# First attention of an eight-sequence transformer: when the loads that fill the stacked queries and keys are issued, and what the long loads and zeros wait for

## The reference, cut to what matters

```
q, k, v = (x @ W.T + b), 16 heads of 8;  heads 0-7 and 8-15 form two groups
a  = softmax(q k^T * 8**-0.5)                         # 512 x 512 per head and sequence
out = concat([x1 - lv * x2, x2]) @ Wp.T + bp          # first attention
top-2 of 8 experts with capacity, pre * silu(gate)    # first expert layer
causal attention, 16 heads of 64                      # second attention
top-4 of 8 experts and a shared expert                # second expert layer
```

## Time and profile before

| | before |
|---|---|
| timed, median of 3 (range) | 1605.11 us (1603.35 to 1608.68) |
| profiled execution, its time | 1597.47 us |
| its span, first to last instruction | 1596.1 us |
| PE busy | 1491.6 us (93%) |
| DVE busy | 1085.2 us (68%) |
| ACT busy | 953.4 us (60%) |
| first attention, about | 52 to 505 us of the span |

### The profile page before, as it was taken

How to read it: one execution, slowest core, us unless ns; L and a number is a source line. 1 busy time by engine, 2 the same in 40 slices (tenths; PEclk the granted TensorE clock), 3 DMA queues, 4 the chain that set the end, 5 groups by cost and what they waited for, 6 DMA issues and landing times.

```text
span 1596.1 us, 26780 instructions
## 1 busy us (share of the span) xinstructions
PE 1491.6 (93%) x8976; PEld 886.4 (56%) x8976; DVE 1085.2 (68%) x3464; ACT 953.4 (60%) x2490; POOL 757.9 (47%) x1250
## 2 busy tenths in 40 slices
PE   4899898899898999998999999999999999998999
PEld 2333333333334999986556565656555565655566
DVE  5887898898793577644776767676777777673333
ACT  4577677777675433444776667575776757573221
POOL 7313354454435677564553646363554534342332
PEclk7798999999998999999999999999999999999999
DMA  6557764683514566872000000000000000020322
GB/s 152 68 125 128 121 138 94 104 134 112 84 35 163 172 194 211 268 234 73 5 12 1 15 1 15 1 15 1 8 8 3 13 1 2 1 54 1 93 67 53
DMA packets 76029, 118.95 MB, mean 75 GB/s; under 512 B 18795, under 2 KB 39533, under 8 KB 75885
## 3 DMA queue, kind: packets, MB, share of 16 engines
q0 software_dynamic: 33952, 67.69, 20.1%
q1 hardware_dynamic: 41504, 48.76, 10.8%
q10 hardware_dynamic: 436, 0.79, 0.2%
HBM read 77.84 MB, written 39.45 MB: 73 GB/s over the span
## 4 chain that ended last, share of the span: by engine, by line
PE 59%; DVE 14%; ACT 10%; DMA 8%; POOL 5%; issue 3%; ACTq 0%; POOLq 0%; DVEq 0%
PE bank L1344 6%; ACT ar L1572 6%; PE pS L1311 5%; DMA dm<-xT 5%; PE bank L1324 4%; DVE mx L1733 4%; PE bank L1353 4%; PE bank L1154 3%; PE pS L1230 3%; PE bank L1244 3%; PE pS L1125 3%; PE pS L1231 3%; PE bank L1281 3%; PE bank L1296 3%; PE bank L1392 3%
## 5 line engine op out<-in xcount | busy, mean ns | idle before, releaser
L2373 POOL TENSOR_SCALAR ar<-ar,rd 128x512 f32<-128x512 f32 (+3 forms) x512 | 264.1, 536 | 307.4 <-DVE rd L2105 307.1
L1572 ACT ACTIVATE ar<-ar,nm 128x512 f32<-128x512 f32 (+3 forms) x512 | 284.9, 558 | 165.0 <-DVE nm L2096 164.8
L1733 DVE TENSOR_REDUCE mx<-pS 128x1 f32<-128x512 f32 x512 | 323.3, 681 | 61.8 <-PE pS L1125 61.8
L1482 ACT ACTIVATE ar<-bank 128x512 f32<-128x512 f32 x342 | 196.5, 599 | 73.8 <-PE bank L1145 66.6
L2096 DVE CUSTOM_DVE_ANT_0 ar<-pS,maskf 128x512 f32<-128x512 f32 (+3 forms) x512 | 228.3, 483 | 17.1 <-PE pS L1311 15.2
L1125 PE MATMUL pS<-all_r 64*128 64x512 f32 x512 | 214.8, 494 | 5.8 <-DVE mx L1733 4.2
L1324 PE MATMUL bank<-identr,all_r 128*128 128x128 f32 x1280 | 199.9, 286 | 11.8 <-ACT ar L1582 6.9
L1324 PEld LDWEIGHTS bank<-identr,all_r 128*128 128x128 f32 x1280 | 132.4, 141 | 111.9 <-issue 79.1
L1125 PEld LDWEIGHTS pS<-all_r 64*128 64x128 f32 x512 | 92.7, 199 | 149.6 <-DVE mx L1733 142.6
L1311 PE MATMUL pS<-ar 64*128 64x512 f32 (+3 forms) x1024 | 172.7, 456 | 0.0
L1145 PE MATMUL bank<-all_r 64*128 64x512 f32 x342 | 150.4, 479 | 12.3 <-DMA all_r<-dm 11.5
(11 more groups left out here) (285 smaller groups left out, 2783.4 us busy)
## 6 DMA issues: line engine op xcount, KB each, us to landing
rows_in<-zrow SPq DMA_DIRECT2D x16, 1024.0 KB, 4.3
ar<-gd SPq DMA_DIRECT2D x16, 512.0 KB, 6.5
all_r<-dk POOLq DMA_DIRECT2D x28, 256.0 KB, 9.7
dk<-xT SPq DMA_DIRECT2D x21, 256.0 KB, 3.2
dq<-xT SPq DMA_DIRECT2D x16, 256.0 KB, 2.9
rows_out<-ar SPq DMA_DIRECT2D x32, 128.0 KB
all_r<-dq POOLq DMA_DIRECT2D x14, 288.0 KB, 6.6
all_r<-dq POOLq DMA_DIRECT2D x14, 256.0 KB, 4.5
```

Source lines behind the costliest of these rows:

```text
L1482: S.activation(pt[n % NPT], bST[n % 3], ACT.Exp, scale=QK_SCALE).then_inc(*s_ex.inc(Gr, kb, j))
L1572: S.activation(p, p, ACT.Exp, bias=nm1[:, c:c + 1], scale=-1.0, accum_out=den1[:, c:c + 1]).then_inc(*s_e1.inc(u, a))
L1733: V.tensor_reduce(mx[Gr % 2][:, col:col + 1], bS[n % 3], AX.X, ALU.max, negate=True).then_inc(*s_mx.inc(Gr, c))
L2373: G.tensor_scalar(p, p, rd1[:, c + a:c + a + 1], 1.0, ALU.mult, ALU.mult).then_inc(*s_p1.inc(u, a))
```

## The change

The stacks of the next batch are issued at steps 1, 2 and 6 in place of 0 and 2. The late loads and the clears wait on SP until the shift of a given group has landed.

```diff
-            for m, when in enumerate((0, 0, 2, 2, 2, 2, 2, 2)):
+            for m, when in enumerate((1, 2, 2, 2, 2, 2, 6, 6)):
                 if when == at:
                     add("stack", b + 1, m)
...
-                add("late", 2 * (3 * b + g - 1) + kb - 2)
+                add("late", 2 * (3 * b + g - 1) + kb - 2, Gr)
...
-        def late(n):
-
+        def behind_land(Gr):
+
+            SP.wait_ge(*a_ms[Gr % 2].at(2 * (Gr // 2 + 1)))
+
+        def late(n, Gr):
+
+            behind_land(Gr + 1)
...
         def clear(b, half):
             SP.wait_ge(*s_id.at("zrow"))
+            behind_land(min(4 * b + 3 + half, NG - 1))
```

## The result

| | before | after |
|---|---|---|
| timed, median of 20 (range) | 1604.56 us (1597.16 to 1614.9) | 1610.68 us (1604.56 to 1618.8) |
| ratio after / before | | 1.0044 (95% interval 1.0028 to 1.0059) |
| span of the profiled execution | 1596.1 us | 1612.8 us |
| first write of batch 1 to first write of batch 7, same execution | 343.4 us | 354.2 us |

By the ratio the changed kernel is 7 us slower (4.5 to 9.5), 0.44%; the plain difference of the two medians is 6.1 us. The two profiled executions lie 17 us apart. That is not the change's price: from one execution to the next both kernels spread over 14 to 18 us, and of before one of the fastest was profiled.

A forecast was written before the change was run, and what follows sets the result against it. PE was taken to be bound by waits for the shift's landing, late behind stacks. Terms 5.0 + 1.7 + 0.5 - 2.1 - 1.5 = +3.6 us gave 1601.1 us for the profiled execution, 1608.7 us timed; range 1598 to 1617.

The forecast's parts named there:

- rival B: Stacks 6 and 7 share DMA engines with transfers SP held back; PE idles 4 to 6 us each time; 1616 us, chance 0.33.
- Parts 1 to 4: Stacks in the first attention: earlier writes against a new wait for stack 7, +5.0 us; slower PE clock, +1.7 us.
- Part 1: First write of dm: stack 1 no longer ahead, 2.6 us sooner in batches 0, 1, 2, 4, 6; nothing in 3, 5.
- Part 4: PE's clock after the wait for stack 7: batches 2 and 5 each lose 0.9 us, +1.7 us in all.
- Part 2: Between the two writes of dm: five stacks behind the landing in place of six, second write lands 2.3 us sooner.
- Part 5: Held-back late loads and clears: cost 0.5 us; last batch gains 2.1 at its landing, 1.5 by clock; other gains excluded.
- rival A: Stack 0 comes behind the first write, the six stacks run in one piece; -11 us in five batches, 1598 us, chance 0.2.
- Rival C: The skill page's DMA estimate holds for two stacks alone, so the new wait is covered; 1582 us, chance 0.05.

The follow-up runs named there:

- one_moved: The kernel before with stacks at step 1, then seven at step 2, without the new waits on SP; ratio to before 0.9959 (-6.7 us).
- four_by_sp: The changed kernel with stacks 4 to 7 issued by SP at step 1, stacks 0 to 3 by POOL at 1, 2, 2, 2; ratio to before 1.0097.
- eight_by_sp: The changed kernel with all eight stacks of sequences 1 to 7 issued by SP at step 1, behind the first write; ratio to before 1.0255.

## Why the prediction was right, and where its terms were off

The exchange of waits, its place (the scores behind the first exp of Gr 4b + 2) and its size (stack 7 lands 7.7 to 8.1 us after the landing's issue, seven times) came as forecast, and the time, 1610.7 against 1608.7 us, lies inside the range. PE stood idle 4.2 to 4.9 us in six batches and 2.1 us in batch 5, where 3 to 5 was forecast. The move of 0.44% is a little over the bound of 0.3%, so slower came, to which I gave 0.36, and not same, to which I gave 0.39. By the ratio the move lies about halfway from my sum (+3.6) to that of rival B (+11), but B's mechanism did not come: it wanted stack 7 over 8.5 us behind the landing's issue. That the total is so near is in part luck, since both halves were off, one to each side.

Parts 1 to 4, the stacks: forecast +5.0 and +1.7, together +6.7 us; measured +8.3 (5.5 to 11.2). The path held in detail. In batch 4 POOL issued the first landing 4.1 us after the first write (forecast 3.6), the second 18.8 (forecast 18.2), and the scores came at 27.0 (forecast 26.3). The first writes gained 2.1, 2.9, 1.4, 2.0 and 2.2 us in batches 0, 1, 2, 4 and 6 (forecast 2.6 each), but in batches 1 and 2 they still took 5.3 and 5.9 us, not near 3.3, since they had taken 8.3 and 7.3 before, more than in batch 4. Part 1's remark on batch 5 held too: nothing won, +1.0 (forecast +0.7). Batch 3 was forecast at +2.8 and measured +1.9 in the first pair of profiles; its second profile of before was 3 us longer, which I could not see from one trace.

Part 4, the clock, was mis-sized: +0.9 us was charged to batches 2 and 5 alone, on the ground that the others ran slow already. In before that was so in batches 3 and 4, not in batch 1. From the scores to the next first write, batches 1 to 5, the mean is 31.4 and 31.9 us in the two profiles of before and 32.4 and 32.3 in those of after, so 0.4 to 1.0 us a batch. In the first pair most of it is in batches 2 (+1.4) and 5 (+2.2). In after the clock stood at its 1.2 GHz level for 3.2 to 6.8 us behind the scores in all ten of these batches, in before in five of ten. How long it stayed there did not follow the idle ahead of it: 6.6 us after 2.1 us of idle (batch 5), 3.2 after 4.2 (batch 3).

Part 2 took 2.3 us for a stack between the writes. With five in place of six the issues of the two landings lay 14.0 to 14.7 us apart in batches 1 to 6, against 16.1 to 18.8 (first pair of profiles), so about right. For seven it is wrong: in one_moved they lay 16.7 us apart on average, against 17.2 and 17.7 in the two profiles of before. So a price for each stack wherever it stands does not carry beyond this change.

Part 5, late loads and clears: forecast +0.5 - 2.1 - 1.5 = -3.1 us; measured -5.4 (-9.3 to -1.6). The sign was right for a reason that did not come. The last landing took 4.33 us before and 3.18 after, where 2.3 was forecast, so the wait at Gr 31 shrank by 1.2 us and not 2.1 (1.5 in the second pair). The slow stretch behind it, of which I took half as spared, grew: in the row below (columns of the earlier trace rows) the first 52 products take 15.6 us at half the clock; in before they take 14.4, at 0.57.

```profile
502.74:518.30 15.56, 15.04 (x52) 4.21 (x52) 3.23 (x17) 8.60 (x17) 11.59 (x19) 0.50 0.87 316
```

So the last batch gave nothing that the profiles show, and the 5.4 us come from the batches before it, where a gain was excluded. That was the error. It comes in part from the order of a clear, the `dq` writes and stack 0, which was priced only as rival A; in batch 1 this was worth some 3 us. The rest is open.

Rival C fell: stacks 6 and 7, alone behind the landing, landed 7.7 to 8.1 us after its issue in all seven batches.

## What to carry to other kernels

When one wait is shortened by issuing other transfers later, find the first reader of those transfers and put its time beside the wait that goes; here the reader stood 0.1 us behind it, and 8.1 us replaced 2.96. A small transfer on a critical path should be issued ahead of bulk loads on every queue, since another queue did not protect it. And run the smaller part of a rearrangement too: moving three stacks lost 8 us, while moving one of them alone gained 7, where the prices said 0 to 2.

## What the runs showed of the hardware that was not expected

- An 8 KB load on POOL's queue took 2.0 to 2.3 us in most landings of after, 8.5 us with four 256 KB loads of SP's queue in flight and 15 us with eight (batch 4 of four_by_sp, batch 3 of eight_by_sp).
- A 256 KB stack costs about 2 us on SP's queue as on POOL's (7.25, 9.19, 11.37 and 13.26 us after the first write in batch 6 of four_by_sp).
- A 16 KB write behind six stacks had its last packet start 5.6 us after its issue, and landed 1.1 us later; the packets themselves were late, and not only the semaphore.
- Seven stacks behind the landing ran to their end in 15.1 and 15.9 us on average, six in 15.4 and 16.1, five in 12.7 and 12.2.
